# Expert outputs moved to the next block's gelu, in an attention stage that is written out instead of looped

## The reference

```python
attn = jnp.einsum('bhqd,bhkd->bhqk', query, key) / scale
attn = jax.nn.softmax(attn, axis=-1)
out = jnp.einsum('bhqk,bhkd->bhqd', attn, value)
...
h = jnp.einsum('bei,eih->beh', jnp.concatenate([merged, ones], -1), w1)
h = jax.nn.gelu(h, approximate=False)
o = jnp.einsum('bej,ejo->beo', jnp.concatenate([h, ones], -1), w2)
```

## Time and profile before

| | us |
|---|---|
| median of 3 runs | 2973.69 (2972.17 to 2976.72) |
| the profiled execution, its time | 2973.5 |
| the profiled execution, its span | 2971.8 |
| TensorE busy, mean granted clock | 2569.5, 0.941 |
| VectorE busy | 2307.5 |
| ScalarE busy | 2025.9 |
| GpSimd busy | 2068.6 |
| start of group 0 to the end of group 15 | 395.35 to 960.18 |

### The profile page before, as it was taken

The page is one execution under the profiler, slowest core; times in us unless marked ns, Lnnn a source line. Parts: engine busy times, 40 slices in busy tenths (PEclk is TensorE's granted clock), DMA queues, the critical chain, the costliest instruction groups (busy, mean ns, idle before and its releaser), DMA issues. The chain is left out here.

```text
span 2971.8 us, 39206 instructions
## 1 busy us (share of the span) xinstructions
PE 2569.5 (86%) x13290; PEld 1485.8 (50%) x13290; DVE 2307.5 (78%) x2777; ACT 2025.9 (68%) x3268; POOL 2068.6 (70%) x650
## 2 busy tenths in 40 slices
PE   5876288888887669999999999999999999999977
PEld 2333133333333435665655655656656556566455
DVE  6576476656562359899899898998998998989985
ACT  3221145556565369788798888897887988888864
POOL 0454441000000159999999999999999999999996
PEclk9998579999899779999999999999999999999989
DMA  8334398767650232132231320321322313213210
GB/s 274 102 105 126 102 264 205 199 165 197 169 166 10 93 121 96 40 122 77 74 122 44 107 112 25 122 100 49 122 72 79 122 37 114 102 35 121 93 51 8
DMA packets 133884, 322.69 MB, mean 109 GB/s; under 512 B 13233, under 2 KB 89009, under 8 KB 117314
## 3 DMA queue, kind: packets, MB, share of 16 engines
q1 hardware_dynamic: 113186, 248.84, 27.4%
q0 software_dynamic: 19200, 70.73, 7.2%
q10 hardware_dynamic: 1312, 0.66, 0.1%
HBM read 277.12 MB, written 43.13 MB: 108 GB/s over the span
## 5 line engine op out<-in xcount | busy, mean ns | idle before, releaser
L1449 DVE TENSOR_TENSOR_SCAN l_st<-l_p_a,l_hl,l_st 128x512 f32<-128x512 f32 x768 | 932.5, 1266 | 106.1 <-ACT l_p_a L1708 95.2
L1630 POOL TENSOR_TENSOR l_st<-l_st,l_cs 128x2048 f32<-128x2048 f32 x192 | 871.5, 4567 | 0.0
L1708 ACT ACTIVATE l_p_a<-l_dt,lw_a_neg 128x512 f32<-128x512 f32 x1024 | 664.8, 680 | 45.2 <-DVE keep_xg L1449 37.0
L1622 POOL TENSOR_TENSOR l_st<-l_bs,l_dtu 128x2048 f32<-128x2048 f32 x128 | 584.4, 4566 | 29.7 <-PE l_p_y L1979 27.5
L1979 PEld LDWEIGHTS l_p_y<-keep_ident,l_st 128*128 128x128 f32 x3072 | 354.1, 144 | 143.7 <-POOL l_st L1630 77.0
L1979 PE MATMUL l_p_y<-keep_ident,l_st 128*128 128x128 f32 x3072 | 384.3, 281 | 48.0 <-POOL l_st L1630 47.8
L969 ACT ACTIVATE a_pr<-a_p_s 128x512 f32<-128x512 f32 x512 | 284.5, 596 | 161.6 <-PE a_p_s L1035 143.7
L893 DVE TENSOR_REDUCE a_mpart<-a_p_m 128x1 f32<-128x512 f32 x512 | 315.2, 683 | 97.7 <-PE a_p_m L1000 95.8
L1449 DVE TENSOR_TENSOR_SCAN keep_xg<-l_p_a,l_hl,keep_xg 128x512 f32<-128x512 f32 x256 | 314.8, 1267 | 1.6
L1630 POOL TENSOR_TENSOR keep_xg<-keep_xg,l_cs 128x2048 f32<-128x2048 f32 x64 | 292.5, 4570 | 2.0 <-ACT l_hl L1713 2.0
L1035 PE MATMUL a_p_s<-a_qst,kx 99*128 99x256 bf16 x1024 | 204.2, 289 | 74.1 <-ACT a_pr L969 55.1
(11 more groups left out here) (225 smaller groups left out, 3920.7 us busy)
## 6 DMA issues: line engine op xcount, KB each, us to landing
a_w<-in_w_dram POOLq DMA_DIRECT2D x64, 1024.0 KB, 11.9
l_bs<-s_bc SPq DMA_DIRECT2D x64, 1024.0 KB, 4.7
l_cs<-s_bc SPq DMA_DIRECT2D x64, 1024.0 KB, 4.8
keep_share<-s_x SPq DMA_DIRECT2D x32, 512.0 KB, 4.9
s_kp<-t_kp SPq DMA_DIRECT2D x96, 128.0 KB
kx<-s_kp SPq DMA_DIRECT2D x16, 768.0 KB, 11.1
s_vp<-t_vo SPq DMA_DIRECT2D x16, 544.0 KB
a_vg<-s_vp SPq DMA_DIRECT2D x16, 544.0 KB, 11.9
```

The source lines that it names most:

```text
L1449: eng.tensor_tensor_scan(st[k % NG][:, n, :], p_a[:, n, :], st[k % NG][:, n, :], hl[:, k, n:n + 1], ALU.mult, ALU.add).then_inc(scan_ok, 1)
L1622: eng.tensor_tensor(st[n][:, :, :], bs[:, 4 * n:4 * n + 4, :], dtu[(k // NG) % 2][:, :].unsqueeze(1).broadcast_to([P, NG, TT]), ALU.mult). ...
L1630: eng.tensor_tensor(st[n][:, :, :], st[n][:, :, :], cs[:, 4 * n:4 * n + 4, :], ALU.mult).then_inc(cm_ok, 1)
L1708: eng.activation(p_a[:, n, :], dt[c % 2][:, :], ACT.Exp, scale=a_neg[:, c, m:m + 1]).then_inc(dA_ok, 1)
```

## The change

Five things change, all in `attention_stage`:

1. `passes` writes all 16 groups out; there is no loop and no register in an address or a wait.
2. `outputs` of quad q leaves group 2q + 1 and goes to group 2q + 3, into chunk 1 behind its second pair of scores. That is beside the gelu of quad q + 1. The outputs of quad 7 have no later gelu: they come at chunk 3 of group 15, which has those of quad 6 at chunk 1.
3. `gl` goes; `hT` has two buffers, and the gelu writes in place.
4. The copy of the outputs to `eo` goes from ScalarE to VectorE, between the eighth and the ninth row maximum of the group that follows (for the last two quads, behind all maxima).
5. The stores of `eo` go from ScalarE's queue to GpSimd's, each behind the load of the next `w2`. That load still waits for the outputs of the quad before.

```diff
@@ passes
-            for hg in range(HG):
-                step(hg, 0, hg)
-            with eng.Fori(1, B) as b:
-                for hg in range(HG):
-                    step(b * HG + hg, b, hg)
+            for g in range(G):
+                step(g, g // HG, g % HG)
@@ gpsimd
+                def load_first(q):
                     wait(eng, h_ok, q)
...
+                def load_second(q):
                     wait(eng, o_ok, q)
...
+                def store(q):
+                    eng.wait_ge(eo_ok, q + 1)
+                    for j in range(4):
+                        eng.dma_start(scr["oe"][:, q * 4 + j, :], eo[32 * j:32 * j + B, :]).then_inc(eo_out, 16)
+
+                load_first(0)
+                load_second(0)
+                load_first(1)
+                for q in range(1, QUADS):
+                    if q + 1 < QUADS:
+                        load_first(q + 1)
+                    load_second(q)
+                    store(q - 1)
+                store(QUADS - 1)
+                eng.wait_ge(eo_out, 64 * QUADS)
@@ vector, maxima
+                        if i == 8 and hg % 2 == 0 and g > 2:
+                            experts_out(g // 2 - 2)
...
+                def experts_out(q):
+                    eng.wait_ge(o_ok, q + 1)
+                    wait(eng, eo_out, q * 64)
+                    eng.tensor_copy(eo[:, :], p_e[:, 0:D]).then_inc(eo_ok, 1)
...
+                def last():
+                    experts_out(QUADS - 2)
+                    experts_out(QUADS - 1)
+                    take(G - 1, B - 1, HG - 1)
@@ scalar
                     eng.wait_ge(hT_ok, q + 1)
-                    eng.activation(hg_t, hT[:, :, :, :], ACT.Gelu).then_inc(hg_ok, 1)
+                    eng.activation(hT[q % 2][:, :, :, :], hT[q % 2][:, :, :, :], ACT.Gelu).then_inc(hg_ok, 1)
-
-                def experts_out(q):
-                    eng.wait_ge(o_ok, q + 1)
-                    wait(eng, eo_out, q * 64)
-                    eng.activation(eo[:, :], p_e[:, 0:D], ACT.Copy).then_inc(eo_ok, 1)
-                    eng.wait_ge(eo_ok, q + 1)
-                    for j in range(4):
-                        eng.dma_start(scr["oe"][:, bass.ds(q * 4 + j, 1), :].rearrange("b a n -> b (a n)"),
-                                      eo[32 * j:32 * j + B, :]).then_inc(eo_out, 16)
...
-                        if c == 2 and hg % 2:
-                            experts_out(b * QB + hg // 2)
@@ tensor, weigh
+                            if c == 1 and hh == 1 and hg % 2 and g > 1:
+                                outputs(b * QB + hg // 2 - 1)
...
-                        if c == 2 and hg % 2:
-                            outputs(b, hg)
+                        if c == 3 and g == G - 1:
+                            outputs(QUADS - 1)
```

More of the change, by code:

```diff
@@ L798, in attention_stage @@
         hraw = sb("hraw", [P, HID])
-        hT = sb("hT", [P, 8, 4, B])
-        gl = sb("gl", [P, 8, 4, B])
+        hT = [sb(f"hT{p}", [P, 8, 4, B]) for p in two]
         eo = sb("eo", [P, D])
@@ L829, in prev @@
         def prev(g, b, hg):
-            return (g - 1, b if hg else b - 1, (hg - 1) % HG)
+            return g - 1, (g - 1) // HG, (g - 1) % HG
         def early(b, hg):
-            return isinstance(b, int) and b == 0 and hg < 2
+            return b == 0 and hg < 2
         with nc.Block() as block:
@@ L851, in load @@
                                   .rearrange("o p c n -> (o p) c n")).then_inc(g_in[hg], 16)
-                    if isinstance(g, int) and g == 0:
+                    if g == 0:
                         eng.dma_start(b1[:, :, :], ins["b1T"]).then_inc(consts, 16)
@@ L861, in _ @@
                     eng.memset(kst[h][R:RM, :, :, :], 1.0).then_inc(ones_ok, 1)
[L863 to L866, removed]
+                def load_first(q):
                     wait(eng, h_ok, q)
                     for j in range(4):
-                        eng.dma_start(w1[:, j, :, :], ins["w1"][bass.ds(q * 4 + j, 1), 0:D, :]
-                                      .rearrange("a (k p) n -> p (a k) n", p=P)).then_inc(w1_in, 16)
+                        eng.dma_start(w1[:, j, :, :], ins["w1"][q * 4 + j, 0:D, :].rearrange("(k p) n -> p k n", p=P)).then_inc(w1_in, 16)
+                def load_second(q):
                     wait(eng, o_ok, q)
                     for j in range(4):
-                        eng.dma_start(w2[:, j, :, :], ins["w2"][bass.ds(q * 4 + j, 1), 0:HID, :]
-                                      .rearrange("a (k p) n -> p (a k) n", p=P)).then_inc(w2_in, 16)
-                passes(eng, quad)
+                        eng.dma_start(w2[:, j, :, :], ins["w2"][q * 4 + j, 0:HID, :].rearrange("(k p) n -> p k n", p=P)).then_inc(w2_in, 16)
+                def store(q):
[12 more added lines that the diff above has]
+                eng.wait_ge(eo_out, 64 * QUADS)
             @block.vector
@@ L921, in step @@
                         eng.wait_ge(hTp_ok, q + 1)
-                        wait(eng, hg_ok, q)
+                        wait(eng, o_ok, q - 1)
                         for k in two:
-                            i = eng.tensor_tensor(hT[:, 4 * k:4 * k + 4, :, :],
+                            i = eng.tensor_tensor(hT[q % 2][:, 4 * k:4 * k + 4, :, :],
                                                   p_m[2 + k][:, :].rearrange("p (c j e) -> p c j e", c=4, j=4)[:, :, :, 0:B],
@@ L928, in step @@
                         i.then_inc(hT_ok, 1)
-                    if not (isinstance(g, int) and g == 0):
+                    if g:
                         take(*prev(g, b, hg))
-                passes(eng, step, lambda: take(G - 1, B - 1, HG - 1))
+                def last():
+                    experts_out(QUADS - 2)
+                    experts_out(QUADS - 1)
+                    take(G - 1, B - 1, HG - 1)
+                passes(eng, step, last)
             @block.scalar
@@ L971, in exps @@
                             gelu(b * QB + hg // 2)
-                        if c == 2 and hg % 2:
-                            experts_out(b * QB + hg // 2)
                 def step(g, b, hg):
-                    if not (isinstance(g, int) and g == 0):
+                    if g:
                         exps(*prev(g, b, hg), following=(g, b, hg))
                     negT(g, b, hg)
-                hg_t = gl[:, :, :, :]
                 passes(eng, step, lambda: exps(G - 1, B - 1, HG - 1))
-                eng.wait_ge(eo_out, 64 * QUADS)
             @block.tensor
@@ L1004, in transpose_max @@
                     eng.wait_ge(np_ok, g + 1)
-                    if hg % 2 == 0:
-                        wait(eng, eo_ok, b * QB + hg // 2)
+                    wait(eng, eo_ok, (g - 2) // 2)
                     for zm in range(8):
@@ L1070, in turned, with outputs @@
                     i.then_inc(hTp_ok, 1)
-                def outputs(b, hg):
-                    q = b * QB + hg // 2
+                def outputs(q):
+                    wait(eng, eo_ok, q)
                     eng.wait_ge(w2_in, q * 64 + 64)
@@ L1077, in outputs @@
                         for j in range(4):
-                            i = eng.matmul(p_e[32 * j:32 * j + B, 0:D], gl[:, c, j, :], w2[:, j, c, :], start=c == 0, stop=c == 7)
+                            i = eng.matmul(p_e[32 * j:32 * j + B, 0:D], hT[q % 2][:, c, j, :], w2[:, j, c, :], start=c == 0, stop=c == 7)
                     i.then_inc(o_ok, 1)
                 def step(g, b, hg):
-                    if isinstance(g, int) and g == 0:
+                    if g == 0:
                         scores(g, b, hg, range(NM))
```

## The result

The changed kernel takes 2901.28 us (median of four runs, 2896.80 to 2905.16); the kernel before took 2974.74 in its four (2972.17 to 2976.72). The ratio is 0.9753, with a 95% interval of 0.9736 to 0.9770. That is 73.5 us less; the forecast was 2902.5. How close the total came is luck: the stage that the change touches gained less than the sum said, and what made up for it lies outside the stage.

A forecast was written before the change was run, and what follows sets the result against it. No engine was the bound but a chain between TensorE and ScalarE, with losses at outputs, gelu and loop. Terms 71.0 + 6.75 - 6.7 = 71.0 us off 2973.5 gave 2902.5, range 2896 to 2911.

The forecast's parts named there:

- The written-out code and the outputs: Groups 3 to 14: writing out the loop and placing outputs beside the gelu gain 71.0 us, odd groups 30.1, even 29.87.
- rival 1: TensorE's clock still falls beside the gelu, or VectorE falls behind: 16 us less gain, 2918 us; chance 0.18.
- VectorE, cost zero with 2 to 3 us of slack: Copy on VectorE between maxima: 0.42 us, hidden, with 2 to 3 us left before the turning at chunk 7.
- 0.1 us longer each: VectorE's row maxima: if each ran this much longer, 2.4 us of slack would go and the cost begin to show.
- Stores from GpSimd, cost zero: Stores on GpSimd's queue: about 51 us of DMA work fit in the 60 us of two groups, nothing late.
- Group 1, 6.75 us less: Group 1, which no longer has any outputs, gains their whole cost of 6.75 us and takes 29.3.
- The 1.65 us: Cost in each of six groups if TensorE's clock still drops beside the gelu; put into the range.
- The last group, 6.7 us lost: Group 15: TensorE waits nearly 8 us for quad 7's w2, outputs then take 5.3; ends at 966.9 instead of 960.2.
- the 15.0: Time in us from outputs ready to w2 landed, read from DMA shares in group 13 and used for group 15.
- Rival 2: The last group does not lose, w2 being there sooner or outputs at chunk 3 cheap: 2896 us; chance 0.08.
- Rival 3: Outputs cost the same wherever they stand: six groups keep 5.95 us each, 36 us less gain, 2938; chance 0.05.
- Rival 4: Written-out code does not come in fast enough, stalls of 5.5 to 5.7 us each, near 3108 us; chance 0.02.

The follow-up runs named there:

- the fourth experiment: The changed kernel with the copy to eo and its four stores back on ScalarE, behind chunk 1's exponentials (chunk 3's for quad 7): 2908.99 us.
- the third experiment: The changed kernel with the outputs left at their old place behind chunk 2 of their own group, copy on VectorE, stores on GpSimd: 2920.02 us.
- the first experiment: The kernel before with all 16 groups written out and nothing else changed: 2945.43 us.
- the repeated run: The changed kernel measured once more, unchanged, beside the fifth, sixth and seventh of the further kernels: 2897.85 us.
- fifth experiment: The changed kernel with quad 7's w2 loaded early into w1's buffer, with a semaphore of its own: 2889.32 us.
- the seventh run: The changed kernel with twelve more row maxima on VectorE ahead of each copy to eo, into a spare tile: 2928.95 us.
- the second experiment: The kernel before with b = 0 and 1 written out and b = 2 and 3 looped, one jump back instead of two: 2964.76 us.

## Why the prediction was right, step by step

**The written-out code and the outputs, 71.0 us in groups 3 to 14.** Measured 70.3. Odd groups take 30.22 against 30.1 predicted, even ones 29.87 as predicted, and ScalarE's loss is 0.79 against 0.8. The sum was made from one group of before, with no split; the runs give one, in the order in which the parts were added: writing out 31.4, the copy and stores off ScalarE 14.1, the place of the outputs 24.8. Another order would share it out otherwise, as the fourth experiment shows for the second part.

**The parts were worth more together than group 1 showed.** By the prediction's own rows writing out alone would leave odd groups at 36.0; they came to 35.9 and 37.5, because TensorE's clock fell at the gelu gap, and in every other odd group behind the stores as well. The prediction took the clock for a side matter, a term of its range; by the third experiment it is about a third of what the place of the outputs is worth. With both gaps gone the granted clock is 1.00, which is what I counted on; the first part of rival 1 did not happen.

**VectorE, cost zero with 2 to 3 us of slack.** The cost is right for the copy, but the slack was in the wrong place, and smaller. The turning had 1.5 us: the last of the steps behind the maxima ran from 517.65 to 517.82, and TensorE's first turning matmul began at 519.36. The slack that decides is some 0.3 us in chunk 2, where a PSUM buffer has to come free. The sentence that named "0.1 us longer each" as the edge was too easy: 1.0 us in one place already costs 0.4 a group. No term of the sum hung on it.

**Stores from GpSimd, cost zero.** Right. The odd group's DMA share is 1.04 and the even one's 0.67, and no engine's rows show a wait for the loads before group 15.

**Group 1, 6.75 us less.** It gained 5.0. With its outputs gone and none put in, the gelu gap stayed open: TensorE waits 2.71 us at 438.95, and the values behind it run at half clock. ScalarE, group 1 of the changed kernel:

```profile
440.45 0.60 ACT L977 ACTIVATE a_pr<-a_p_s 128x512 f32<-128x512 f32 x1 [0.26 <-PE a_p_s L1038]
442.94 2.33 ACT L977 ACTIVATE a_pr<-a_p_s 128x512 f32<-128x512 f32 x4 [1.90 <-PE a_p_s L1038]
```

In group 3 there is 0.88 of idle time at the same place. The 1.65 us that the prediction priced for a clock that falls, and left out of the sum, was due here. In group 1 of before the clock stayed at 1.00 over a gelu gap of the same length (434.60 to 442.60) and fell behind the stores (0.64 from 448.23 to 453.03). So 4.80 - 3.27 = 1.53 of the 6.75 was half clock (with the clock at 1.00 there, in group 3 of the first experiment, that step takes 3.26), and in group 1 it did not go with the outputs but came at the other gap.

**The last group, 6.7 us lost.** The mechanism was right and the size was not: it lost 9.6, and 7.5 in the repeated run (42.3 - 34.8). Taking `w2` away from it (fifth experiment) took 12.3 us out of the group. TensorE in group 15 of the changed kernel:

```profile
857.00 3.64 PE L1083 MATMUL a_p_e<-a_w,a_hT 128*4 128x256 f32 x64
...
877.56 6.13 PE L1083 MATMUL a_p_e<-a_w,a_hT 128*4 128x256 f32 x64 [9.63 <-issue]
```

The first outputs end at 860.64, 8.9 after the group's start at 851.75, where the prediction had 934.2 - 925.37 = 8.8. The term that was too small is the 15.0 from there to the landing of `w2`, which the prediction read from the DMA share. The share falls to 0.75 in the window up to 876.00, so most of the bytes are in 15.0 us after the outputs; but the next window still moves 10 GB/s, and the matmuls wait for the last transfer. When it landed stands beside its line. GpSimd's four transfers, group 13 of before and group 15 of the changed kernel:

```profile
L874 POOL DMA_DIRECT2D a_w<-in_w_dram x4: 882/886/894, 876.4 to 879.1; - x4
DMA to landing us min/median/max: 6.6/11.0/14.1
...
L866 POOL DMA_DIRECT2D a_w<-in_w_dram x4: 884/898/913, 861.0 to 863.9; - x4
DMA to landing us min/median/max: 6.3/9.9/13.6
```

The last one of before landed at 879.1 + 14.1 = 893.2, that is 17.3 us after the outputs at 875.88 and not 15.0. With 17.3 the prediction's own sum would have had a wait of 10.0 us. In the changed kernel it landed at 863.9 + 13.6 = 877.5, 16.9 after the outputs, and TensorE starts at 877.56. So it waits 9.63 instead of nearly 8. The outputs then run for 6.13 us instead of 5.3, with the clock at 0.50 after the long wait. In the repeated run the landing comes after 15.8 us, the wait is 8.60 and the outputs take 5.04. The trace names the wait "issue"; that it is the wait for `w2` was shown by the fifth experiment, in which it is gone. The Trainium skill's page "DMA: Bandwidth & Descriptors", by which the prediction estimated 11.6 us for the same stretch, is further off than the 15.0: the traces have 17.3, 16.9 and 15.8.

**The total.** In the stage the sum was 71.0 and 64.4 came, or 66.4 in the repeated run: 6.6 and 4.6 us short, from group 1, group 15 and group 0. The medians differ by 73.5 all the same. Of the 9 us beyond the stage, 4.4 are the part behind it in this profiled execution (in the repeated run that part took 3.7 more), and most of the rest comes from the profiled execution being the slowest of the four, 2905.16 against the median of 2901.28. So the agreement to 1.2 us is chance. The stage's gain of some 65 us alone would put the kernel near 2908, still inside the forecast's own range of 2896 to 2911.

**The rivals.** Rival 1 is out for the changed kernel (the clock stays, VectorE is in time), but the seventh run shows that it was near: with 4.06 us on VectorE it costs 4.7 a group. Rival 2, no loss in the last group, is what the fifth experiment makes of it; it came to 2889.3, below the 2896 I gave it, since group 15 then takes 32.1 us, 2.7 less than before the change. Rival 3 would have left odd groups at 36.0; they are 30.2. Rival 4 is out: with a DMA share of 1.04, and three packets of code in group 3 as in group 1 of before, the longest stand of TensorE or its weight loads on "issue" between groups 0 and 14 is 0.9 us. The Trainium skill's rule that a taken branch out of the fetched code stalls ("Runtime: NRT & Kernel Launch", "Instruction fetch mechanics") agrees again with the second experiment: one jump is left, and one stand, of 5.58 us.

## What to carry to other kernels

Work on TensorE that must come somewhere belongs where TensorE already waits for a serial step elsewhere. Here that gap cost twice, 2.7 us as time and on average 1.4 as the clock behind it, so filling it gave 4.1 us for outputs that take 3.6.

When work goes to an engine that "has slack", find the first place at which another engine waits for one of its buffers, and measure there. With four rotating buffers the slack was 0.3 us, while that at the end of the row looked like 2 to 3.

Before a pipeline is shifted by a stage, look at its two ends: the first group had nothing to fill its gap, and the last got two portions with a load between them. A buffer that is already free there gave back 12.3 us (10.2 against the repeated run), more than the forecast loss of 6.7. And when a step waits for a load, read when its last transfer landed, not when the DMA share falls: here 2 us lie between.

## What the runs showed of the hardware

- A jump back cost 8.1 us in the kernel with one of them, and 6 to 8 in the kernel before, not the 5.5 to 5.7 of its stand alone; TensorE comes out of it at half clock (0.50 from 774.23 to 777.60).
- The same two idle times of TensorE per odd group (2.7 and 1.5 us) lowered the clock once in one group and twice in the next, by turns: 0.95 and 0.91, 35.9 and 37.5 us. With the outputs at their old place and the copy gone from ScalarE, one gap of 2.7 us left the clock at 1.00 in one odd group and lowered it in five. Why was not tried.
- Four small stores hold ScalarE's next activation for 1.42 to 1.46 us with constant addresses and 2.28 with addresses from registers. On GpSimd's queue the same four take 2.05 us to start:

```profile
864.76 2.05 POOL L871 DMA_DIRECT2D s_oe<-a_eo  x4
```

- Four transfers of 1 MB, issued one behind the other, had all landed 15.8 to 17.3 us after the matmul that freed their buffer, and TensorE's first matmul began within 0.1 us of the last landing (877.5 and 877.56, 875.0 and 875.07 in the repeated run). The DMA share had fallen some 2 us earlier in two of these three, while a last trickle was still on its way.
- The second layer, the same instructions each time, took 2005.7 to 2015.3 us in the profiled executions. Differences of a few us between two kernels are better read from the stage that was changed than from the total.
